# Query bound moved from ScalarE to VectorE, and one large SiLU with its reduction cut into eight, in a transformer layer on eight cores

## The chip, the cores and the metric

The kernel runs on one Trainium2 chip, on all 8 of its cores. Each core computes two of the sixteen sequences by itself; there is no exchange between cores. The metric is the device time of the slowest core, in microseconds (us), lower is better.

## The reference

The layer is an attention block and a feed-forward block, each between two layer norms, for x of shape (16, 2048, 1024). Cut to what matters:

```python
q, k, v = x@wq + bq, x@wk + bk, x@wv + bv              # 16 heads of 64
att = softmax(q @ k.T / 8) @ v
x = x + layernorm(att @ wo.T + bo)                     # x was layernorm(x) before q, k, v
# feed-forward on layernorm(x):
h = bit_linear(x, w1)                                  # 1024 -> 4096, x quantised per token, w1 ternary
h = silu(depthwise_conv1d(h, conv_w, conv_b))          # 3 taps along the sequence
# bit_linear's act_quant: scale = 127 / clip(max |h| over 4096); round(h * scale)
x = x + layernorm(bit_linear(h, w2))                   # 4096 -> 1024
```

## The kernel before, in words

Each core does a weight statistic once (`_p0`), and then for each of its two sequences: layer norm (`_p1_ln1`), the q, k and v projections (`_p2_qkv`), attention (`_p3_attn`), output projection and two layer norms (`_p4_proj_ln`), weight quantisation (`_p45_wquant`) and the feed-forward (`_p5_ffn`). Every stage writes one stream of instructions per engine. `em.emit` appends an instruction to its engine's stream with the semaphore values that it waits for, and every VectorE and ScalarE instruction also waits for the one before it on its own engine. The order on an engine is the order of the `emit` calls, and nothing reorders it.

**Attention (from line 439).** Heads go one after the other. In a head, 16 key blocks (`kt`) times 2 query halves (`j`) pass through a chain: scores on TensorE into `sc0` or `sc1` (line 514), exponential on ScalarE into `pt` (line 527), product with v on TensorE into `atps` (line 540). A score block waits for the exponential that last read its buffer. The exponential needs an upper bound of the scores, which comes from |q|: `emit_absq` (line 481) puts |q| of the next head into `absq`, `emit_M` (line 487) multiplies it with the maxima of |k|, and VectorE writes the negated bound into row 64 of `qa` (line 497). `absq` is the tile `oddh`, which also holds the finished output of odd heads (`ctx["absq"] = oddh`).

When a head ends, VectorE copies `atps` to `ivr`, which is the tile `ivfm` (line 549), and takes the reciprocal of its row 64, the softmax sums (line 557). The rest of the old head's work stands in the next head ahead of `kt` 7: `emit_post(h - 1)` (line 563) spreads the reciprocals over 64 partitions by TensorE (line 570) into `sc0` and `sc1`, and VectorE multiplies (line 581). For an even old head the product goes to `attn` (printed as `s_big`), for an odd one to `oddh`, from where a DMA moves it into `attn` (line 585, semaphore `sod`). `emit_absq(h + 1)` stands right behind this, and the score block of `kt` 7 waits for the multiplies (`mult_done`).

**Feed-forward (from line 789).** The sequence goes in 16 tiles of 128 tokens. In a tile, 32 blocks of 128 channels are computed: 8 matmuls per block on TensorE (line 842) into one of two PSUM tiles `hps`, which VectorE scales into `hgr` (line 854). TensorE can be two blocks ahead, since it waits for `hevac[idx - 2]`. After every fourth block VectorE does the convolution of these four in six operations (lines 879 to 889) into 512 of the 4096 columns of `tcv`. When all eight groups are done, ScalarE does SiLU on the whole of `tcv` (line 891), VectorE takes the maximum of the absolute value over the 32 blocks (line 893), and the scale comes from it by way of TensorE (lines 896 to 917). Then GpSimd and VectorE quantise the eight groups, and TensorE multiplies each with `w2q` (line 958).

## Time and profile before

| What | us |
|---|---|
| Runs: median of 2, and both | 7871.88 (7823.92, 7919.83) |
| The profiled execution, its own time | 7823.42 |
| Its span, first to last instruction, slowest core | 7821.4 |
| Shortest span of the eight cores | 7791.7 |
| VectorE busy, slowest core | 4261.6 |
| TensorE busy | 3709.8 |
| ScalarE busy | 1264.3 |
| GpSimd busy | 674.7 |

The profiled execution is 2 us outside its span and 48 us under the median of the two runs. The eight cores do the same work, and their spans lie within 30 us. No engine is busy for much over half of the span, so shares of busy time alone do not say what bounds the kernel; the stages have different limits and have to be read one by one.

### The profile page before, as it was taken

To read this page: it belongs to the slowest core of one execution; us is meant where nothing else is said; L and a number is where in the kernel's file an instruction comes from. 1 tells how busy PE (TensorE), PEld (TensorE's weight loads), DVE (VectorE), ACT (ScalarE), POOL (GpSimd) and SP (SyncE) were. 2 spreads that over 40 slices of the span, in tenths; PEclk is the share of its full clock that TensorE was granted. 3 is DMA by queue.
4 is the path that set the end of the run, shared out by engine and by line. 5 is a ranking of instruction groups with operands and counts; after the bars stand their busy time and mean duration, and the time that the engine had idled before them with its cause. 6 is when DMAs were issued, how large, how long until landed. Compare 5 with 4: busy or idle time off the path is not lost. (4 is left out here: it accounts for less than half of the span.)

```text
span 7821.4 us, 57703 instructions; the slowest of 8 cores (7791.7 to 7821.4 us)
## 1 busy us (share of the span) xinstructions
PE 3709.8 (47%) x17510; PEld 1786.6 (23%) x17510; DVE 4261.6 (54%) x5764; ACT 1264.3 (16%) x1226; POOL 674.7 (9%) x629
## 2 busy tenths in 40 slices
PE   0688787221144344344416887872224444344441
PEld 0322222110132232222203222221112222222220
DVE  4333443557666666666653334345546666666665
ACT  0046665000000000000000466650000000000000
POOL 0000000000012112112110000000002112112121
PEclk9987777565566666666658877775656666666665
DMA  6200000113400000000042000001120000000004
GB/s 191 60 6 6 9 9 5 50 38 110 158 6 6 3 6 6 3 6 3 6 156 52 7 5 8 9 5 50 38 97 6 3 6 4 5 6 3 6 6 132
DMA packets 59118, 251.86 MB, mean 32 GB/s; under 512 B 6720, under 2 KB 6848, under 8 KB 55232
## 3 DMA queue, kind: packets, MB, share of 16 engines
q1 hardware_dynamic: 40992, 197.32, 8.0%
q0 software_dynamic: 17824, 50.86, 2.4%
q8 instruction: 147, 2.41, 0.1%
q14 instruction: 155, 1.27, 0.1%
HBM read 185.77 MB, written 67.11 MB: 32 GB/s over the span
## 5 line engine op out<-in xcount | busy, mean ns | idle before, releaser
L842 PE MATMUL s_hps<-s_xqfm,s_w1q 128*128 128x130 bf16 (+1 forms) x8192 | 866.6, 293 | 1142.8 <-DVE s_hgr L854 768.8
L527 ACT ACTIVATE s_pt<-s_sc 128x1024 bf16<-128x1024 f32 x1024 | 1048.7, 1024 | 470.4 <-PE s_sc L514 401.5
L842 PEld LDWEIGHTS s_hps<-s_xqfm,s_w1q 128*128 128x128 bf16 x8192 | 777.9, 134 | 1240.0 <-issue 1219.6
L958 PE MATMUL s_fp<-s_w2q,s_gq 128*128 128x512 bf16 x2048 | 715.5, 512 | 713.8 <-DVE s_gq L947 713.8
L514 PE MATMUL s_sc<-s_qa,s_ka 65*128 65x512 bf16 x2048 | 774.4, 470 | 176.7 <-ACT s_pt L527 64.6
L540 PE MATMUL s_atps<-s_pt,s_vsb 128*65 128x512 bf16 x2048 | 691.8, 436 | 0.2 <-ACT s_pt L527 0.2
L891 ACT ACTIVATE s_tcv<-s_tcv 128x4096 bf16<-128x4096 bf16 x32 | 115.7, 3616 | 3454.7 <-DVE s_tcv L889 3454.7
L941 DVE SCALAR_TENSOR_TENSOR s_f<-s_db,s_r 128x512 f32<-128x512 f32 x256 | 395.6, 1545 | 406.9 <-POOL s_db L938 406.9
L929 POOL TENSOR_TENSOR s_yb<-s_tcv,s_sgb 128x512 f32<-128x512 bf16 x256 | 296.0, 1156 | 3539.4 <-DVE s_sgb L917 3507.3
L854 DVE SCALAR_TENSOR_TENSOR s_hgr<-s_hps,iwcol,s_ivfm 128x130 bf16<-128x130 f32 (+1 forms) x1024 | 361.4, 353 | 430.8 <-PE s_hps L842 371.4
L549 DVE COPY s_ivfm<-s_atps 65x2048 f32<-65x2048 f32 x32 | 73.2, 2286 | 845.2 <-PE s_atps L540 845.2
L958 PEld LDWEIGHTS s_fp<-s_w2q,s_gq 128*128 128x128 bf16 x2048 | 227.0, 119 | 1188.5 <-issue 1106.5
L557 DVE RECIPROCAL s_ivfm<-s_ivfm 1x2048 f32<-1x2048 f32 x32 | 414.2, 12944 | 3.3
L938 POOL TENSOR_TENSOR s_db<-s_yb,s_r 128x512 f32<-128x512 f32 x256 | 323.0, 1262 | 616.5 <-DVE s_r L935 616.5
L514 PEld LDWEIGHTS s_sc<-s_qa,s_ka 65*128 65x128 bf16 x2048 | 170.9, 108 | 742.8 <-issue 728.5
L540 PEld LDWEIGHTS s_atps<-s_pt,s_vsb 128*65 128x65 bf16 x2048 | 258.2, 127 | 312.2 <-issue 149.2
L716 PE MATMUL s_trp<-eye16s,s_xqt 128*128 128x128 bf16 x256 | 32.4, 306 | 604.2 <-DVE s_xqt L260 604.2
L893 DVE TENSOR_REDUCE s_gmax<-s_tcv 128x128 f32<-128x4096 bf16 x32 | 223.5, 6986 | 128.8 <-ACT s_tcv L891 128.8
L896 PE MATMUL s_tmp<-eye32s,s_gmax 128*128 128x128 f32 x32 | 14.3, 447 | 511.2 <-DVE s_gmax L893 511.2
L375 PE MATMUL s_qps<-s_big,s_xqfm 128*128 128x512 bf16 x1024 | 224.6, 383 | 39.5 <-DMA s_xqfm<-wq_t 39.5
L244 ACT ACTIVATE sdc<-st 128x1 f32<-128x1 f32 x128 | 25.9, 203 | 1159.1 <-DVE st L239 1159.0
L667 PE MATMUL s_op<-s_wo,s_big 128*128 128x512 bf16 x512 | 176.5, 521 | 41.1 <-DMA s_wo<-wo_t 41.1
(118 smaller groups left out, 3698.1 us busy)
## 6 DMA issues: line engine op xcount, KB each, us to landing
s_xint<-x SPq DMA_DIRECT2D x64, 512.0 KB, 4.1
p0st<-w_t SPq DMA_DIRECT2D x8, 2048.0 KB, 10.0
p0st<-w_t SPq DMA_DIRECT2D x32, 512.0 KB, 3.7
x2scr<-s_x2t SPq DMA_DIRECT2D x32, 512.0 KB, 2.9
s_wst<-w_t SPq DMA_DIRECT2D x16, 1024.0 KB, 5.1
s_wst<-w_t SPq DMA_DIRECT2D x32, 512.0 KB, 3.7
fscr<-s_ft POOLq DMA_DIRECT2D x32, 512.0 KB, 3.0
s_frl<-fscr SPq DMA_DIRECT2D x32, 512.0 KB, 5.9
```

The lines of the kernel that those rows point to most:

```text
L375: wo=wofs[wb]: e.matmul(ps[:, nb * 512:(nb + 1) * 512], wtens[:, wo + dc * D + oc * 128:wo + dc * D + oc * 128 + 128], xn1[:, dc * S + nb ...
L514: em.emit("tensor", lambda e, kt=kt, nb=nb, b=b, j=j: e.matmul(scp[j][:, nb * 512:(nb + 1) * 512], ka[:, b * S + kt * 128:b * S + kt * 128 ...
L527: em.emit("scalar", lambda e, p=p, j=j: e.activation(pt[:, p * S + j * Q:p * S + (j + 1) * Q], scp[j][:], AF.Exp), waits=w)
L540: em.emit("tensor", lambda e, kt=kt, nb=nb, h=h, p=p, j=j: e.matmul(atps[0:65, j * Q + nb * 512:j * Q + (nb + 1) * 512], vsb[:, kt * VW + ...
L557: em.emit("vector", lambda e: e.reciprocal(ivr[64:65, :], ivr[64:65, :]))
L842: j0=j0, j1=j1, t0=t0: e.matmul(ps[:, j0:j1], w1q[:, dc * DH + cc * 128:dc * DH + cc * 128 + 128], xqfm[:, dc * S + t0 + j0:dc * S + t0 + j1],
L854: t0=t0: e.scalar_tensor_tensor(hgr[:, gb + c4 * 130 + j0:gb + c4 * 130 + j1], ps[:, j0:j1], sb["iwcol"][:, 0:1], ivfm[:, t0 + j0:t0 + j1] ...
L893: em.emit("vector", lambda e: e.tensor_reduce(gmax[:], rearr(tcv, "p (c t) -> p t c", c=HC), AX.X, ALU.max, apply_absolute_value=True), wa ...
L929: em.emit("gpsimd", lambda e, ts=ts: e.tensor_tensor(rearr_ap3(yb), rearr_ap3(ts), sgv, ALU.mult), inc=ctx["gc"], waits=yw)
L938: em.emit("gpsimd", lambda e: e.tensor_sub(db2[:], yb[:], r02[:]), inc=ctx["gc"], waits=[(dv, r0d)])
L941: em.emit("vector", lambda e: e.scalar_tensor_tensor(f12[:], db2[:], 1.5, r02[:], ALU.is_gt, ALU.add), waits=[(ctx["gc"], dg)])
L958: gq4=gq4, cc4=cc4: e.matmul(ps[:, nb * 512:(nb + 1) * 512], gq4[:, cc4 * 128:(cc4 + 1) * 128], w2q[:, cc * D + nb * 512:cc * D + (nb + 1) ...
```

## The change

In attention, |q| is no longer one ScalarE activation (`Abs`) but two VectorE operations, a multiplication by -1 and a maximum. They stand at the same place in the order of the code, with the same waits for the DMAs `sqa` and `sod`. `emit_M` waits for a named exponential of the head before instead of for the newest ScalarE instruction. After the reciprocal, VectorE also copies row 64 to a bf16 row `ivb16` in the tile `xqfm`; nothing reads this copy, and the matmul of line 570 still reads the fp32 row with `ones32`. The new tile `ones16` isn't read either.

In the feed-forward, SiLU and the maximum are done per group of 512 columns, right behind the group's convolution: eight activations and eight reductions instead of one of each, and seven maxima that join the partial results. The two lines about `silu_ac` near the end give the variable the value that it had.

```diff
+    sb["ones16"] = nc.alloc_sbuf_tensor("ones16", [128, 128], BF16)
...
+                    ctx["ivb16"] = xqfm
...
-            em.emit("scalar", lambda e, b=b: e.activation(
-                absq[0:64, :], qa[0:64, b * S:(b + 1) * S], AF.Abs),
-                waits=[(sqa, None), (sod, None), (dv, None)])
+            em.emit("vector", lambda e, b=b: e.tensor_scalar_mul(
+                absq[0:64, :], qa[0:64, b * S:(b + 1) * S], -1.0),
+                waits=[(sqa, None), (sod, None)])
+            em.emit("vector", lambda e, b=b: e.tensor_tensor(
+                absq[0:64, :], absq[0:64, :], qa[0:64, b * S:(b + 1) * S],
+                ALU.max))
...
-                    waits=([(dv, None), (ac, None)] if nb == 0 else []))
+                    waits=([(dv, None), (ac, exp_cnt.get((h - 1, NT - 1, j), 0))]
+                           if nb == 0 else []))
...
             em.emit("vector", lambda e: e.reciprocal(
                 ivr[64:65, :], ivr[64:65, :]))
+            em.emit("vector", lambda e: e.tensor_copy(
+                ctx["ivb16"][64:65, 0:S], ivr[64:65, :]))
...
                     convd.append(dv.n)
-            em.emit("scalar", lambda e: e.activation(tcv[:], tcv[:], AF.Silu),
-                    waits=[(dv, None)])
-            em.emit("vector", lambda e: e.tensor_reduce(
-                gmax[:], rearr(tcv, "p (c t) -> p t c", c=HC), AX.X, ALU.max,
-                apply_absolute_value=True), waits=[(ac, None)])
+                    g_ = cc // 4
+                    em.emit("scalar", lambda e, g_=g_: e.activation(
+                        tcv[:, g_ * 512:(g_ + 1) * 512],
+                        tcv[:, g_ * 512:(g_ + 1) * 512], AF.Silu),
+                        waits=[(dv, None)])
+                    em.emit("vector", lambda e, g_=g_: e.tensor_reduce(
+                        gmax[:] if g_ == 0 else f12[:, 0:128],
+                        bass.AP(tcv, g_ * 512, [[HC * 128, 128], [1, 128],
+                                                [128, 4]]),
+                        AX.X, ALU.max, apply_absolute_value=True),
+                        waits=[(ac, None)])
+                    if g_ > 0:
+                        em.emit("vector", lambda e: e.tensor_max(
+                            gmax[:], gmax[:], f12[:, 0:128]))
...
+            del silu_ac
+            silu_ac = ctx["ac"].n
```

VectorE's order in the feed-forward, one group of a tile, before (the brackets name the semaphores that an instruction waits for: `pe` TensorE, `dv` VectorE, `ac` ScalarE):

```order
L854 SCALAR_TENSOR_TENSOR s_hgr<-s_hps,iwcol,s_ivfm 128x130 [waits pe,dv] x4
L879 TENSOR_TENSOR s_tcv<-s_hgr,cw_sb 128x512 [waits dv]
L881 TENSOR_TENSOR s_tcv<-s_tcv,cb_sb 128x512 [waits dv]
L883 TENSOR_TENSOR s_tmpg<-s_hgr,cw_sb 128x512 [waits dv]
L885 TENSOR_TENSOR s_tcv<-s_tcv,s_tmpg 128x512 [waits dv]
L887 TENSOR_TENSOR s_tmpg<-s_hgr,cw_sb 128x512 [waits dv]
L889 TENSOR_TENSOR s_tcv<-s_tcv,s_tmpg 128x512 [waits dv]
L854 SCALAR_TENSOR_TENSOR s_hgr<-s_hps,iwcol,s_ivfm 128x130 [waits pe,dv] x4
```

The same group in the changed kernel, whose lines are numbered differently (863 for 854, 888 to 898 for 879 to 889):

```order
L863 SCALAR_TENSOR_TENSOR s_hgr<-s_hps,iwcol,s_ivfm 128x130 [waits pe,dv] x4
L888 TENSOR_TENSOR s_tcv<-s_hgr,cw_sb 128x512 [waits dv]
L890 TENSOR_TENSOR s_tcv<-s_tcv,cb_sb 128x512 [waits dv]
L892 TENSOR_TENSOR s_tmpg<-s_hgr,cw_sb 128x512 [waits dv]
L894 TENSOR_TENSOR s_tcv<-s_tcv,s_tmpg 128x512 [waits dv]
L896 TENSOR_TENSOR s_tmpg<-s_hgr,cw_sb 128x512 [waits dv]
L898 TENSOR_TENSOR s_tcv<-s_tcv,s_tmpg 128x512 [waits dv]
L905 TENSOR_REDUCE s_f<-s_tcv 128x128 [waits ac,dv]
L912 TENSOR_TENSOR s_gmax<-s_gmax,s_f 128x128 [waits dv]
L863 SCALAR_TENSOR_TENSOR s_hgr<-s_hps,iwcol,s_ivfm 128x130 [waits pe,dv] x4
```

A reduction that waits for ScalarE, and a maximum, have come between the convolution of one group and the first read of `hps` of the next.

VectorE's order in attention from the start of an odd head (the copy out of `atps` of the even head before it) to the multiplies, before:

```order
L549 COPY s_ivfm<-s_atps 65x2048 [waits pe,dv]
L497 TENSOR_SCALAR s_qa<-s_sc 1x1024 [waits pe,dv] x2
L467 COPY s_qa<-s_qpk 64x2048 [waits dv]
L467 COPY s_ka<-s_kpk 64x2048 [waits dv]
L475 TENSOR_REDUCE s_mke<-s_ka 64x1 [waits dv]
L557 RECIPROCAL s_ivfm<-s_ivfm 1x2048 [waits dv]
L581 TENSOR_TENSOR s_big<-s_ivfm,s_sc 64x1024 [waits pe,dv] x2
```

And in the changed kernel, where 556 stands for 549, 504 for 497, 470 for 467, 478 for 475, 564 for 557 and 590 for 581:

```order
L556 COPY s_ivfm<-s_atps 65x2048 [waits pe,dv]
L504 TENSOR_SCALAR s_qa<-s_sc 1x1024 [waits pe,dv] x2
L470 COPY s_qa<-s_qpk 64x2048 [waits dv]
L470 COPY s_ka<-s_kpk 64x2048 [waits dv]
L478 TENSOR_REDUCE s_mke<-s_ka 64x1 [waits dv]
L564 RECIPROCAL s_ivfm<-s_ivfm 1x2048 [waits dv]
L566 CAST s_xqfm<-s_ivfm 1x2048 [waits dv]
L590 TENSOR_TENSOR s_big<-s_ivfm,s_sc 64x1024 [waits pe,dv] x2
L487 TENSOR_SCALAR s_oddh<-s_qa 64x2048 [waits dv]
L490 TENSOR_TENSOR s_oddh<-s_oddh,s_qa 64x2048 [waits dv]
```

The copy (L566) has come between the reciprocal and the multiplies, and the two operations that make |q| stand behind the multiplies. In the heads where the old head is odd, the first of these two waits for `sqa` and `sod` as well. On ScalarE nothing but exponentials is left in this stage.

## Rows read from the trace of the kernel before

**Rows 1.** The page's busy time, share of the span and instructions of each engine.

```profile
PE 3709.8 (47%) x17510; PEld 1786.6 (23%) x17510; DVE 4261.6 (54%) x5764; ACT 1264.3 (16%) x1226; POOL 674.7 (9%) x629
```

**Rows 2.** Windows, first sequence: attention, feed-forward. Columns: us, then busy per engine, PEclk, DMA share.

```profile
453.00:1382.00 929.00, 731.25 (x2240) 236.83 (x2240) 372.31 (x129) 556.20 (x529) 4.11 (x2) 0.78 0.03 7
2088.00:3835.00 1747.00, 741.66 (x4719) 467.52 (x4717) 1102.11 (x1787) 55.52 (x16) 298.55 (x254) 0.66 0.02 7
```

**Rows 3.** Timeline, feed-forward group and tile's end: start, us, engine, line, operation, idle before.

```profile
2671.39 3.63 PE L842 MATMUL s_hps<-s_xqfm,s_w1q 128*128 128x130 bf16 x32 [3.64 <-DVE s_hgr L854]
2672.59 0.35 DVE L854 SCALAR_TENSOR_TENSOR s_hgr<-s_hps,iwcol,s_ivfm 128x130 bf16<-128x130 f32 x1 [0.89 <-PE s_hps L842]
...
2707.05 0.43 DVE L889 TENSOR_TENSOR s_tcv<-s_tcv,s_tmpg 128x512 bf16<-128x512 bf16 x1
2707.62 3.62 ACT L891 ACTIVATE s_tcv<-s_tcv 128x4096 bf16<-128x4096 bf16 x1 [114.82 <-DVE s_tcv L889]
2711.41 6.99 DVE L893 TENSOR_REDUCE s_gmax<-s_tcv 128x128 f32<-128x4096 bf16 x1 [3.93 <-ACT s_tcv L891]
2718.54 0.45 PE L896 MATMUL s_tmp<-eye32s,s_gmax 128*128 128x128 f32 x1 [15.84 <-DVE s_gmax L893]
```

**Rows 4.** Groups of instructions by line and shape: busy us, mean ns, idle before.

```profile
L893 DVE TENSOR_REDUCE s_gmax<-s_tcv 128x128 f32<-128x4096 bf16 x32 | 223.5, 6986 | 128.8 <-ACT s_tcv L891 128.8
L885 DVE TENSOR_TENSOR s_tcv<-s_tcv,s_tmpg 128x512 bf16<-128x512 bf16 x256 | 108.7, 425 | 27.6 <-DVE s_tmpg L883 1.4
L201 DVE TENSOR_REDUCE t1c<-p0st 128x1 f32<-128x1024 f32 x32 | 39.0, 1220 | 39.9 <-DMA p0st<-w_t 39.8
L201 DVE TENSOR_REDUCE t1c<-p0st 128x1 f32<-128x4096 f32 x8 | 35.4, 4420 | 38.6 <-DMA p0st<-w_t 38.6
L253 DVE CAST s_qi<-s_yq 128x1024 int32<-128x1024 f32 x32 | 22.2, 694 | 3.6 <-DVE s_yq L712 0.5
L891 ACT ACTIVATE s_tcv<-s_tcv 128x4096 bf16<-128x4096 bf16 x32 | 115.7, 3616 | 3454.7 <-DVE s_tcv L889 3454.7
L484 ACT ACTIVATE s_oddh<-s_qa 64x2048 bf16<-64x2048 bf16 x32 | 61.1, 1909 | 217.0 <-DMA s_big<-s_oddh 133.6 <-DVE s_big L581 83.2
```

**Rows 5.** Line 484, what ended ScalarE's idle time before it: us in total, times.

```profile
  DMA s_big<-s_oddh: 133.6, 14
  DVE s_big L581: 83.2, 14
```

**Rows 6.** Timeline of attention, an even head (old head odd), around `kt` 7.

```profile
712.22 1.01 PE L514 MATMUL s_sc<-s_qa,s_ka 65*128 65x512 bf16 x2 [1.54 <-DVE s_oddh L581]
715.15 1.91 ACT L484 ACTIVATE s_oddh<-s_qa 64x2048 bf16<-64x2048 bf16 x1 [8.65 <-DMA s_big<-s_oddh]
724.13 14.41 ACT L527 ACTIVATE s_pt<-s_sc 128x1024 bf16<-128x1024 f32 x13 [0.21 <-PE s_sc L514]
739.46 2.29 DVE L549 COPY s_ivfm<-s_atps 65x2048 f32<-65x2048 f32 x1 [27.39 <-PE s_atps L540]
```

**Rows 7.** Timeline of attention, the odd head behind it (old head even).

```profile
750.52 12.94 DVE L557 RECIPROCAL s_ivfm<-s_ivfm 1x2048 f32<-1x2048 f32 x1
758.09 6.61 ACT L527 ACTIVATE s_pt<-s_sc 128x1024 bf16<-128x1024 f32 x6 [0.38 <-PE s_sc L514]
764.84 4.20 PE L570 MATMUL s_sc<-s_ivfm,ones 1*64 1x512 f32 x8 [1.21 <-ACT s_pt L527]
770.58 1.91 ACT L484 ACTIVATE s_oddh<-s_qa 64x2048 bf16<-64x2048 bf16 x1 [5.88 <-DVE s_big L581]
775.00 17.76 ACT L527 ACTIVATE s_pt<-s_sc 128x1024 bf16<-128x1024 f32 x16 [0.28 <-PE s_sc L514]
```

**Rows 8.** Windows of the same even head: TensorE slow, then fast.

```profile
712.00:723.00 11.00, 8.25 (x20) 2.95 (x21) 0.07 (x1) 6.11 (x6) 0.00 (x0) 0.50 0.11 24
723.00:739.00 16.00, 15.08 (x62) 5.50 (x60) 0.00 (x0) 14.23 (x14) 0.00 (x0) 0.99 0.00 1
```

**Rows 9.** Timeline, the end of the first sequence's attention.

```profile
1373.92 7.05 PE L570 MATMUL s_sc<-s_ivfm,ones 1*64 1x512 f32 x8 [15.65 <-DVE s_ivfm L557]
```

More of the change, by code:

```diff
@@ L180, in _p0 @@
     em.emit("gpsimd", lambda e: e.memset(sb["ones32"][:], 1.0))
+    em.emit("gpsimd", lambda e: e.memset(sb["ones16"][:], 1.0))
     em.emit("gpsimd", lambda e: e.memset(sb["epsc"][:], 1e-5))
```

## The prediction

> **What bounds the kernel now.** Busy time comes first: VectorE is busy for 54% of the span, TensorE for 47%, ScalarE for 16% [rows 1], so no engine bounds the whole. The windows of the two stages that the change touches are next [rows 2]. In attention ScalarE is busy for 556 of 929 us and TensorE for 731. In the feed-forward VectorE has 1102 of 1747 us, TensorE 742, ScalarE 56. The other stages are not touched; I count them at zero.
>
> The timeline then shows what waits for what. In the feed-forward TensorE does the 32 matmuls of a group in 3.63 us and has then waited 3.64 us for VectorE to free `hps` [rows 3]. So groups are 7.27 us apart, all of it VectorE's, and TensorE has half of it as slack. At the tile's end there is a chain with nothing beside it: convolution ends at 2707.48, SiLU starts 0.14 us later, takes 3.62, VectorE starts the reduction 0.17 us behind it, takes 6.99, and only then does TensorE go on [rows 3]. So whatever is put into VectorE's stream here is paid in full.
>
> In attention the limit alternates. With TensorE's granted clock at its upper level (2.4 GHz; 0.99 in the windows) ScalarE bounds: 13 exponentials take 14.41 us, so (14.41 - 1.02) / 12 = 1.116 us each [rows 6, 8]. After the stall at `kt` 7 the clock is at 0.50, 1.2 GHz [rows 8], and TensorE bounds, with four matmuls of 512 columns per exponential, 4 x 512 / 1.2 = 1.71 us.
>
> **The feed-forward, step by step.** What each tile loses from its end is 3.93 us of wait (with SiLU in it) and 6.99 us of reduction [rows 3], 10.92 us. What it gets:
>
> - SiLU of 512 columns. From 3616 ns for 4096 columns and 1909 for 2048 [rows 4] ScalarE takes 0.833 ns per column and 202 ns besides (another function, but the same engine and the same kind of operands): 629 ns. VectorE waits 0.14 + 0.63 + 0.17 = 0.94 us for it. The reduction stands right behind in VectorE's order, and so nothing of VectorE lies beside the wait. 8 x 0.94 = 7.51 us.
> - The reduction of 512 columns to 128. This is the term that no row shows. Contiguous reductions take 1220 ns for 1024 and 4420 ns for 4096 elements [rows 4]: 1.042 ns per element and 153 ns besides. The one of line 893 has 4096 elements too, but takes 6986 ns, 2566 more [rows 4]. It differs in two things: it reads with a step of 256 bytes, and it writes 128 results instead of one. If the step is what costs, an element takes (6986 - 153) / 4096 = 1.668 ns and the small reduction 153 + 512 x 1.668 = 1.01 us. If each result costs 2566 / 128 = 20 ns, it takes 153 + 533 + 2566 = 3.25 us. If neither returns with rows of four, 0.69 us. I take 1.01: both reductions read with the same step, and it is the only reading by which the total of the elements prices both. 8 x 1.01 = 8.06 us. The ends 0.69 and 3.25 are kept.
> - Seven maxima of 128 fp32 elements. The nearest rows are the 425 ns of a bf16 operation on 512 [rows 4] as the upper end, and 153 ns, the fixed part, as the lower. At one element per 1.042 ns it is 0.29 us, with the usual 0.11 us to the next instruction 0.40. 7 x 0.40 = 2.77 us.
>
> The gap of 0.11 us behind the convolution is there before and after. Sum per tile: 7.51 + 8.06 + 2.77 - 10.92 = +7.42 us. Two sequences of 16 tiles: 32 x 7.42 = +237 us. TensorE gives nothing back. It has the next two blocks ready and then waits for `hps`, as now, and the 0.89 us that VectorE waits for the third block [rows 3] comes after VectorE's own read and stays. The clock is already low in this phase (32 matmuls of 130 columns in 3.63 us, 113 ns each, near 130 / 1.2 = 108). By the ends of the reduction it is 32 x (8 x 0.69 - 0.64) = +156 us and 32 x (8 x 3.25 - 0.64) = +812 us.
>
> A page bears on this term. The Trainium skill, SBUF — State Buffer, section "Door 1: The DMA port swizzle", says in a note on cachelines that SBUF has lines of 16 bytes and that an access which crosses to a new line pays a penalty. By that rule every element of either reduction pays, and the small one takes 1.01 us; the 1.668 ns against 1.042 of the trace agree with a price per access, but do not prove it, since the number of results fits as well.
>
> **Attention, step by step.** The activation on |q| leaves ScalarE in the 28 heads where it stands behind a post. The two kinds differ.
>
> - Old head odd, 14 times: ScalarE can't take |q| until the DMA out of `oddh` has landed, at 715.15, though TensorE has restarted at 712.22 and has scores for it [rows 6]. The eighth exponential behind the stall starts at 724.13 + 2 x 1.116 = 726.36, 14.1 us after the restart. With an old even head there is no DMA to wait for, |q| starts when the multiplies are done and TensorE restarts too, and the eighth exponential comes at 775.00 + 5 x 1.116 = 780.58, 10.0 us after 770.58 [rows 7]. Without the activation the first kind can do no worse than the second: 4.1 us less. Some of that is the DMA and the activation, the rest that TensorE isn't interrupted while its clock is low. 14 x 4.1 = 58 us. The mean idle time before the activation, 133.6 / 14 = 9.5 us against 83.2 / 14 = 5.9 us [rows 5], differs by 3.6 us and supports the size.
> - Old head even, 14 times: about nothing. TensorE has just restarted at the low clock and is the bound, so the activation was hidden beside it: the third exponential comes 4.4 us after the restart [rows 7], and TensorE alone needs 1.2 + 2 x 1.71 = 4.6 at the low clock.
> - The first head of each sequence, 2 times, gains some 1.5 us: 3 us.
>
> VectorE's two operations take about 0.7 and 1.2 us (a bf16 operation with two inputs takes 425 ns for 512 elements [rows 4], (425 - 153) x 4 + 153 = 1.24). They stand where VectorE is idle for over 20 us, until `atps` is complete (27.39 us [rows 6]), and there its wait for the DMA is hidden too, as nothing is queued behind it but that copy. If that cover were gone it would be 2 us in each head, 60 us.
>
> The unread copy of the reciprocals stands on the path to the post. The cast of 1024 fp32 elements takes 694 ns [rows 4], so 2048 take 153 + 2 x 541 = 1.23 us, with the gap 1.34. The upper bound is the 2.29 us of the copy from PSUM [rows 6]. The reciprocal ends at 763.46, the exponentials for which the post also waits at 764.70 [rows 7]: 1.24 us of cover, so about 0.1 us is lost in the 14 or so heads of this kind, 2 us. Where the old head is odd there is more cover, since two copies are missing ahead of the reciprocal. At the end of a sequence the post waits for the reciprocal alone [rows 9]: 2 x 1.34 = 3 us. The changed wait of `emit_M` gives nothing, since its `dv` wait includes the copy out of `atps`, which comes after the last exponential anyway.
>
> Attention: -58 - 3 + 2 + 3 = -56 us. Its bounds are wide on one side: 20 us less gain if the clock's recovery doesn't follow, and up to 96 us more (the third rival).
>
> **Sum.** +237 - 56 = +181 us on the profiled execution's 7823.4: 8004 us. That execution lies 48 us under the median of the two runs, and the same sum on the median gives 8053. I forecast 8028, the middle, which is slower by 2.3% of 7823. A measurement of this kernel can tell about 2% from no change, which is 156 us, so the forecast lies only just outside.
>
> **Rivals.**
>
> - Each result of a reduction costs 20 ns. For it: the same 2566 ns. Against it: a cost of 19 VectorE cycles for one result is much for an engine that streams. The feed-forward gives +812, the whole 7823 + 812 - 56 = 8579 us. Chance 0.12.
> - Rows of four run at the contiguous rate. For it: four elements may be fetched differently from 32. Against it: the step is the same. The small reduction takes 0.69 us, and the whole comes to 7823 + 156 - 56 = 7923 us, within 2%. Chance 0.10. The Trainium skill, VectorE: DVE Perf Modes, section "The perf-mode tier table", says that `tensor_reduce` runs at one element per cycle in any memory; by that the small one takes 0.69 us. The trace agrees for line 201 and departs from it for line 893.
> - Not slower: TensorE's clock no longer falls at the stall. ScalarE frees the chain earlier, and if the clock stays up from the restart on, five steps at the low clock (1.71 us against 1.116) become fast in each head, 3 us. 32 x 3 = 96 us more than in the forecast: 7908 us, 1% over before, no difference that counts. It decides from 25 us (0.8 us a head) on. Against it: in the window from 712 to 723 the clock is low already at the restart [rows 8], and the post ahead of it is not shortened. Chance 0.04. Nothing that I can find makes the kernel faster by 2%; for that the feed-forward would have to be unchanged and attention to gain nearly three times its 56 us.
> - The forecast, 0.74.
>
> **How the numbers follow.** Inside the forecast the uncertainty is some 25 us, mostly the clock in attention and which execution is taken as the base; this puts about 0.06 of its 0.74 within 2%. Slower: 0.68 + 0.12 = 0.80. Within 2%: 0.06 + 0.10 + 0.04 = 0.20, less 0.01 for a gain unknown to me. The range goes from 7915, which takes in the second rival, to 8130, and leaves the first out.
>
> **What would show it.** In the changed profile the reductions of 512 elements take 1.01 us (3.25 or 0.69 for the rivals); SiLU takes 0.63 with 0.94 us of idle time ahead of each reduction; the distance between groups in a tile is 7.27 + 0.94 + 1.01 + 0.11 + 0.29 = 9.6 us; attention is 28 us shorter per sequence, and ScalarE's idle time at `kt` 7 of an even head falls from 8.65 to some 6.9 us, since the first exponential comes 1.2 us behind TensorE's restart. The forecast is wrong if SiLU and convolution overlap, if the clock at the restart is 1.00, or if groups are less than 9.3 us apart.

## The result and the profile after

The changed kernel takes 8043.5 us (median of 11 runs, 8024.8 to 8132.6) against 7841.3 (median of 10 runs of the kernel before). The ratio is 1.025, with 1.021 to 1.029 as its interval: slower by 2.5%. The forecast was 8028 us in a range from 7915 to 8130. The profiled execution took 8077.5 us. In it cores 4 to 7 had a lower granted clock (0.674 to 0.677) than cores 0 to 3 (0.691 to 0.694) and took some 45 us longer, for a reason that no run shows, so I compare cores 0 to 3. Core 0's span went from 7821.4 to 8004.6 us, +183.

The page's busy time, of core 6, beside [rows 1]:

```profile
PE 3777.3 (47%) x17510; PEld 1807.2 (22%) x17510; DVE 4463.4 (55%) x6308; ACT 1248.7 (15%) x1418; POOL 675.9 (8%) x630
```

VectorE is busy for 202 us more. That this is near the whole difference is chance, for the new waits for SiLU aren't in it, and in attention VectorE's new work is mostly hidden. The windows of core 0 (attention of the first sequence, a stretch of its feed-forward; columns as in [rows 2]) show TensorE's clock as before, and VectorE in attention with 40 us more, ScalarE with 31 less:

```profile
453.00:1377.00 924.00, 734.14 (x2237) 233.49 (x2236) 412.19 (x170) 525.09 (x513) 0.87 (x1) 0.78 0.04 9
2060.00:4095.00 2035.00, 793.08 (x5072) 501.50 (x5072) 1250.68 (x2205) 80.93 (x131) 321.27 (x276) 0.65 0.03 10
```

The groups of instructions of core 0, by line and shape (busy us, mean ns, idle time before), answer to [rows 4]:

```profile
L905 DVE TENSOR_REDUCE s_f<-s_tcv 128x128 f32<-128x512 bf16 x224 | 227.3, 1015 | 213.9 <-ACT s_tcv L901 213.9
L901 ACT ACTIVATE s_tcv<-s_tcv 128x512 bf16<-128x512 bf16 x256 | 161.0, 629 | 3776.8 <-DVE s_tcv L898 3776.7
L912 DVE TENSOR_TENSOR s_gmax<-s_gmax,s_f 128x128 f32<-128x128 f32 x224 | 65.5, 292 | 23.6 <-DVE s_f L905 0.5
L566 DVE CAST s_xqfm<-s_ivfm 1x2048 bf16<-1x2048 f32 x32 | 39.0, 1218 | 3.3
L490 DVE TENSOR_TENSOR s_oddh<-s_oddh,s_qa 64x2048 bf16<-64x2048 bf16 x32 | 39.0, 1217 | 3.3
L905 DVE TENSOR_REDUCE s_gmax<-s_tcv 128x128 f32<-128x512 bf16 x32 | 32.5, 1015 | 33.2 <-ACT s_tcv L901 33.2
L487 DVE TENSOR_SCALAR s_oddh<-s_qa 64x2048 bf16<-64x2048 bf16 x32 | 21.9, 685 | 44.9 <-DMA s_big<-s_oddh 42.9
```

The small reduction takes 1.015 us, SiLU 0.63, and VectorE waits (213.9 + 33.2) / 256 = 0.965 us for it each time. The maxima take 0.29. The end of one group of the feed-forward in the timeline of core 0 (start, us, then as in [rows 3]) shows them in a row:

```profile
2224.99 0.42 DVE L898 TENSOR_TENSOR s_tcv<-s_tcv,s_tmpg 128x512 bf16<-128x512 bf16 x1
2225.57 0.63 ACT L901 ACTIVATE s_tcv<-s_tcv 128x512 bf16<-128x512 bf16 x1 [9.00 <-DVE s_tcv L898]
2226.37 1.01 DVE L905 TENSOR_REDUCE s_f<-s_tcv 128x128 f32<-128x512 bf16 x1 [0.95 <-ACT s_tcv L901]
2227.49 0.29 DVE L912 TENSOR_TENSOR s_gmax<-s_gmax,s_f 128x128 f32<-128x128 f32 x1
2227.88 0.81 DVE L863 SCALAR_TENSOR_TENSOR s_hgr<-s_hps,iwcol,s_ivfm 128x130 bf16<-128x130 f32 x2
2228.38 1.89 PE L851 MATMUL s_hps<-s_xqfm,s_w1q 128*128 128x130 bf16 x16 [6.00 <-DVE s_hgr L863]
```

Between the end of the convolution, 2225.41, and the next read of `hps`, 2227.88, lie 2.47 us with nothing of VectorE's other work in them. The groups are 9.62 us apart, and TensorE's wait for `hps` has grown from 3.64 [rows 3] to 6.00 us: it is still the engine with slack.

An even head around `kt` 7 (timeline of core 0, answers to [rows 6]):

```profile
692.06 3.94 PE L579 MATMUL s_sc<-s_ivfm,ones 1*64 1x512 f32 x8 [1.21 <-ACT s_pt L534]
697.88 1.01 PE L521 MATMUL s_sc<-s_qa,s_ka 65*128 65x512 bf16 x2 [1.89 <-DVE s_oddh L590]
699.05 1.02 ACT L534 ACTIVATE s_pt<-s_sc 128x1024 bf16<-128x1024 f32 x1 [7.13 <-PE s_sc L521]
700.80 0.69 DVE L487 TENSOR_SCALAR s_oddh<-s_qa 64x2048 bf16<-64x2048 bf16 x1 [3.06 <-DMA s_big<-s_oddh]
702.40 17.75 ACT L534 ACTIVATE s_pt<-s_sc 128x1024 bf16<-128x1024 f32 x16 [0.62 <-PE s_sc L521]
```

The DMA now holds up VectorE, which has nothing else to do. ScalarE starts with an exponential 1.17 us behind TensorE's restart; before, it waited 2.93 us for the DMA and then did |q| first. Its idle time is 7.13 us instead of 8.65. The windows behind this restart (columns as in [rows 2]) show the other half of the gain:

```profile
697.90:699.90 2.00, 2.00 (x5) 0.75 (x6) 0.00 (x0) 0.85 (x1) 0.00 (x0) 0.50 0.48 104
699.90:701.90 2.00, 2.00 (x6) 0.84 (x5) 1.00 (x2) 1.20 (x2) 0.00 (x0) 0.50 0.12 27
701.90:703.90 2.00, 1.98 (x9) 0.76 (x8) 0.90 (x1) 1.41 (x2) 0.00 (x0) 0.96 0.03 8
```

TensorE works without a gap from the restart and is back at 2.4 GHz (0.96 in the window) after 4 us. In the head of [rows 6], on the kernel before, it took 10 us, with two of them idle (windows of that kernel):

```profile
716.20:718.20 2.00, 0.00 (x0) 0.00 (x0) 0.00 (x0) 1.88 (x2) 0.00 (x0) 0.50 0.00 0
722.20:724.20 2.00, 2.00 (x8) 0.83 (x7) 0.00 (x0) 1.10 (x3) 0.00 (x0) 0.71 0.00 0
```

To see where the time went I took the length of each stage from its first and last record: attention from the first copy of keys and queries to the last multiply, the feed-forward from the first read of `hps` to the last write of its output, both sequences together.

| stage, us | before (8 cores) | after (cores 0 to 3) | difference | forecast |
|---|---|---|---|---|
| feed-forward | 3810 to 3819, median 3814 | 4060 to 4064, median 4061 | +247 | +237 |
| attention | 1859 to 1865, median 1862 | 1819 to 1829, median 1824 | -38 | -56 |
| all the rest | 2118 to 2144 | 2106 to 2125 | some -15 | 0 |

The rest moved by as much among kernels in which nothing of it differs (2105 to 2145 us on cores 0 to 3 of all runs), so I take the -15 for the noise of an execution. Attention is 18 us short of its forecast. Per core, an even head (counted from 0; from its first exponential to that of the next head, in the mean of heads 2 to 14) went from 58.5-58.9 to 54.5-54.7 us, as forecast (4.1 less); an odd one (heads 1 to 13) from 54.4-54.6 to 56.1-56.75. Before, an odd head needed 5.8 to 6.1 us from the post's first matmul to the restart of the chain; now 6.8 to 7.4, again in the mean of a core.

### The profile page after: what moved, and what is told of

It reads as the page before. It is cut to its first block and busy times, and to the rows that moved or that the text cites. A ratio compares the mean times of both kernels' runs of the same rounds, so it can differ in the third digit from the quotient of the medians.

```text
span 8075.8 us, 59576 instructions; the slowest of 8 cores (7990.8 to 8075.8 us)
## 1 busy us (share of the span) xinstructions
PE 3777.3 (47%) x17510; PEld 1807.2 (22%) x17510; DVE 4463.4 (55%) x6308; ACT 1248.7 (15%) x1418; POOL 675.9 (8%) x630
## 5 line engine op out<-in xcount | busy, mean ns | idle before, releaser
L901 ACT ACTIVATE s_tcv<-s_tcv 128x512 bf16<-128x512 bf16 x256 | 161.2, 630 | 3778.3 <-DVE s_tcv L898 3778.3
L905 DVE TENSOR_REDUCE s_f<-s_tcv 128x128 f32<-128x512 bf16 x224 | 227.0, 1014 | 213.9 <-ACT s_tcv L901 213.9
L378 PE MATMUL s_qps<-s_big,s_xqfm 128*128 128x512 bf16 x1024 | 247.9, 411 | 38.0 <-DMA s_xqfm<-wq_t 38.0
L579 PE MATMUL s_sc<-s_ivfm,ones 1*64 1x512 f32 x256 | 182.0, 872 | 74.9 <-DVE s_xqfm L566 51.2
```

The costliest lines, as they stand in the source:

```text
L378: wo=wofs[wb]: e.matmul(ps[:, nb * 512:(nb + 1) * 512], wtens[:, wo + dc * D + oc * 128:wo + dc * D + oc * 128 + 128], xn1[:, dc * S + nb ...
L905: em.emit("vector", lambda e, g_=g_: e.tensor_reduce(gmax[:] if g_ == 0 else f12[:, 0:128], bass.AP(tcv, g_ * 512, [[HC * 128, 128], [1, 128],
```

## The experiments

All ratios are to the kernel before, run on the same chip, with the 95% interval behind them. Ranges of a stage are over the eight cores where nothing else is said.

**The two parts apart.** `e3_attention_only` is the changed kernel with the old end of the tile:

```diff
-                    g_ = cc // 4
-                    em.emit("scalar", lambda e, g_=g_: e.activation(
-                        tcv[:, g_ * 512:(g_ + 1) * 512],
-                        tcv[:, g_ * 512:(g_ + 1) * 512], AF.Silu),
-                        waits=[(dv, None)])
...
+            em.emit("scalar", lambda e: e.activation(tcv[:], tcv[:], AF.Silu),
+                    waits=[(dv, None)])
+            em.emit("vector", lambda e: e.tensor_reduce(
+                gmax[:], rearr(tcv, "p (c t) -> p t c", c=HC), AX.X, ALU.max,
+                apply_absolute_value=True), waits=[(ac, None)])
```

> Only the attention part of the change; the feed-forward is that of the kernel before. If the two parts don't act on each other: attention about 1820 us for both sequences (1861 before), feed-forward 1905 us each as before, the kernel 0.5% faster than before (ratio 0.995). If the attention gain of the changed kernel belongs to something else (placement in memory, clock of a die), it stays at 1.000.

Measured 7789.8 us, 0.995 (0.993 to 0.997); attention 1817 to 1836 us, feed-forward 3805 to 3818.

`e4_ffn_only` is the kernel before with that part of the change alone, the reverse of the diff above.

> Only the feed-forward part of the change. Theory: the eight exposed waits, reductions and maxima cost 247 us per core by themselves; feed-forward 2030 us per sequence, attention as before, ratio 1.031. Rival: part of the 247 us comes from the rest of the change (the lower clock of a die, memory placement); then it is under 1.028.

Measured 8048.7 us, 1.027 (1.025 to 1.029); feed-forward 4057 to 4065 us, attention 1854 to 1865. So each part moves its own stage and leaves the other where it was. -0.5% and +2.7% add to +2.2%, beside 2.5% (2.1 to 2.9) for the whole. For the second I had expected 1.031, and had named a ratio under 1.028 as a sign that part of the 247 us comes from elsewhere. The ratio is under it, but the feed-forward grew by its 246 us all the same (4060 against 3814); in the profiled execution it is the untouched stages that were some 15 us shorter again.

**The copy of the reciprocals.** `e1_no_copy` takes it out:

```diff
             em.emit("vector", lambda e: e.reciprocal(
                 ivr[64:65, :], ivr[64:65, :]))
-            em.emit("vector", lambda e: e.tensor_copy(
-                ctx["ivb16"][64:65, 0:S], ivr[64:65, :]))
             ctx[f"_iv{h}"] = dv.n
```

> The changed kernel without the unread bf16 copy of the reciprocals. What is asked: why attention became only 38 us shorter per core (both sequences, undisturbed die) where 56 were forecast. Heads with an even number became 4.3 us shorter, odd ones 1.9 to 2.3 us longer. Theory A: in odd heads the copy ends up to 1.2 us after the exponentials for which the post also waits, and this delay is enough that TensorE's clock is at its lower level for the post, so the copy costs more than its own uncovered time. Then odd heads go back from 56.5 to some 54.5 us, attention (both sequences) from about 1820 to about 1790 us, and the kernel is 2.1% slower than before instead of 2.5%. Rival B: the copy costs only the 0.1 us of the forecast, and attention stays within 5 us of 1820. Rival C: the two |q| operations on VectorE lengthen the odd heads; they stay at 56.5 us.

`e2_copy_behind` keeps it, but emits it in `emit_post`, behind the multiplies:

```diff
             mult_done[h] = dv.n
+            em.emit("vector", lambda e: e.tensor_copy(
+                ctx["ivb16"][64:65, 0:S], ivr[64:65, :]))
```

> The changed kernel with the same copy moved behind the post's multiplies, where VectorE is idle. Theory A (the copy's place between reciprocal and post is what costs): as without the copy, odd heads 54.5 us, attention about 1790 us. If instead the copy costs wherever it stands (VectorE's time, or the write to that tile), attention stays at about 1820 us.

Measured: 7992.9 us, 1.0215 (1.0174 to 1.0256), without the copy, and 7990.1, 1.0193 (1.0175 to 1.0211), with it behind the multiplies. The first interval overlaps that of the changed kernel (1.021 to 1.029), the second ends at its edge. The stages say more: attention is 1793 to 1799 us on cores 0 to 3 of the first and 1793 to 1796 on all cores of the second, against 1819 to 1829. So the copy costs some 30 us where it stands, and nothing where it runs beside TensorE. It is the place, not the 1.22 us of VectorE. Most of it is in the odd heads, 54.8-55.0 us in the first and 54.6-54.9 in the second against 56.1-56.75: 14 x 1.5 = 21 us. The even heads have 0.2 us each, some 3 us, and the first and last heads of the sequences the rest.

How does 1.22 us cost that much, where 0.1 was forecast? An odd head of the changed kernel, core 0 (timeline):

```profile
844.57 12.94 DVE L564 RECIPROCAL s_ivfm<-s_ivfm 1x2048 f32<-1x2048 f32 x1
849.04 8.83 ACT L534 ACTIVATE s_pt<-s_sc 128x1024 bf16<-128x1024 f32 x8 [1.54 <-PE s_sc L521]
857.62 1.22 DVE L566 CAST s_xqfm<-s_ivfm 1x2048 bf16<-1x2048 f32 x1
859.09 7.05 PE L579 MATMUL s_sc<-s_ivfm,ones 1*64 1x512 f32 x8 [2.28 <-DVE s_xqfm L566]
862.91 1.21 DVE L590 TENSOR_TENSOR s_big<-s_ivfm,s_sc 64x1024 bf16<-64x1024 f32 x1 [4.07 <-PE s_sc L579]
866.32 1.21 DVE L590 TENSOR_TENSOR s_big<-s_ivfm,s_sc 64x1024 bf16<-64x1024 f32 x1 [2.20 <-PE s_sc L579]
867.68 1.01 PE L521 MATMUL s_sc<-s_qa,s_ka 65*128 65x512 bf16 x2 [1.54 <-DVE s_big L590]
...
4729.02 12.94 DVE L564 RECIPROCAL s_ivfm<-s_ivfm 1x2048 f32<-1x2048 f32 x1
4736.90 6.60 ACT L534 ACTIVATE s_pt<-s_sc 128x1024 bf16<-128x1024 f32 x6 [0.68 <-PE s_sc L521]
4742.07 1.22 DVE L566 CAST s_xqfm<-s_ivfm 1x2048 bf16<-1x2048 f32 x1
4743.64 3.89 PE L579 MATMUL s_sc<-s_ivfm,ones 1*64 1x512 f32 x8 [1.20 <-ACT s_pt L534]
4745.71 1.21 DVE L590 TENSOR_TENSOR s_big<-s_ivfm,s_sc 64x1024 bf16<-64x1024 f32 x1 [2.43 <-PE s_sc L579]
4747.71 1.21 DVE L590 TENSOR_TENSOR s_big<-s_ivfm,s_sc 64x1024 bf16<-64x1024 f32 x1 [0.78 <-PE s_sc L579]
4749.07 1.01 PE L521 MATMUL s_sc<-s_qa,s_ka 65*128 65x512 bf16 x2 [1.53 <-DVE s_big L590]
```

In the first head the exponentials are done at 857.87, but the copy only at 858.84. The post starts 1.22 us behind the exponentials, after 2.28 us of idle TensorE, and takes 7.05 us; in the second head, 0.14 us behind them, 3.89. From the post to the restart it is 8.59 us in the one and 5.43 in the other. The windows of the two posts (columns as in [rows 2], the clock third from the end) show why:

```profile
859.10:863.10 4.00, 4.00 (x5) 1.15 (x6) 0.19 (x1) 0.00 (x0) 0.00 (x0) 0.50 0.00 0
863.10:867.70 4.60, 3.06 (x5) 0.50 (x4) 2.29 (x3) 0.00 (x0) 0.00 (x0) 0.50 0.00 0
4743.50:4747.20 3.70, 3.56 (x8) 0.98 (x8) 1.21 (x1) 0.00 (x0) 0.00 (x0) 0.95 0.00 0
```

The late post runs at the low level of TensorE's clock, 1.2 GHz, the punctual one mostly at 2.4. The 112 odd heads of the eight cores sort the same way; the mean granted clock during the post is 0.84 in the 46 punctual ones and 0.54 in the 66 others:

| post behind the last exponential | heads | post to restart, us | head, us |
|---|---|---|---|
| up to 0.3 us | 46 | 5.80 | 54.85 |
| 0.3 to 1.0 us | 25 | 7.72 | 57.71 |
| 1.0 to 1.5 us | 41 | 8.33 | 58.16 |

Heads whose post starts 1.0 to 1.5 us behind (1.19 in the mean, where 0.14 is the least) take 3.3 us longer. But neither lateness nor idle time fixes the price by itself. On cores 0 to 3 of this kernel 76 posts behind some 1.2 us of idle TensorE take from 3.89 to 6.08 us, 27 of them over 5, and in `e2_copy_behind` odd heads need 6.3 to 6.65 us from post to restart, where the kernel before needed 5.8 to 6.1, although every post is punctual in both. No run here shows what decides the moment at which the clock falls.

`e9_quarter_copy` makes the copy short and `e10_copy_twice` makes it twice as long:

```diff
-                ctx["ivb16"][64:65, 0:S], ivr[64:65, :]))
+                ctx["ivb16"][64:65, 0:512], ivr[64:65, 0:512]))
```

> The changed kernel with the copy cut to 512 of its 2048 columns (0.42 + 0.11 us instead of 1.22 + 0.11). In odd heads the reciprocal ends about as long ahead of the last exponential as the whole copy takes, so this one should be fully covered if the cost lies in the post starting late: attention near the 1794 us without the copy (within 8), odd heads 54.5 to 55 us. If any instruction between reciprocal and post costs, whatever its length (an extra semaphore step, the other tile), it stays near 1824 us, odd heads 56 us.

```diff
             em.emit("vector", lambda e: e.tensor_copy(
                 ctx["ivb16"][64:65, 0:S], ivr[64:65, :]))
+            em.emit("vector", lambda e: e.tensor_copy(
+                ctx["ivb16"][64:65, 0:S], ivr[64:65, :]))
```

> The changed kernel with the same copy done twice in a row, 2.65 us between reciprocal and post. If the post starting late is the cause, odd heads grow by at least the 1.33 us of the second copy over the changed kernel's 56.5 us, to 57.8 or more, and even heads (cover about 2.8 us) stay within 0.5 us of 54.6: attention 1824 + 14 x 1.33 + 3 = about 1846 us. If the cost came only once from TensorE's clock being low at the post, and not from lateness itself, the second copy costs less than 1 us per head.

There is one execution of each, 8017.8 and 8075.2 us, so I go by the stages. Attention takes 1794 to 1810 us (median 1802) with the quarter, 1859 to 1875 (median 1868) with two: in order of the copy's length (none, a quarter, one, two) 1795, 1802, 1824, 1868. With the quarter 65 odd heads are on time and take 54.6 us, 47 are 0.4 us late and take 55.8. With two copies 87 are 2.36 us late and take 58.7, the other 25 are 1.26 us late and take 57.6 (6.73 us from post to restart, less than the 8.33 of the heads that are 1.19 us late with one copy). So both rivals fall: it is not any instruction whatever its length, and the second copy costs more than 1 us per odd head. It costs 44 us, twice what I expected of it: odd heads lose 2.0 us instead of 1.33, and even heads, which I had taken as covered (at most 0.5 us), about 1 us. The direction is shown by four lengths; the size is not a constant per microsecond.

**The step of the reduction.** `e5_steps` is the kernel before, in which the reduction still reads 4096 elements for 128 results, but with a step that changes from tile to tile, so that the maximum is taken over other columns:

```diff
-            em.emit("vector", lambda e: e.tensor_reduce(
-                gmax[:], rearr(tcv, "p (c t) -> p t c", c=HC), AX.X, ALU.max,
+            em.emit("vector", lambda e, i=i: e.tensor_reduce(
+                gmax[:], bass.AP(tcv, 0, [[HC * 128, 128], [1, 128],
+                                         [2 ** (i % 8), 32]]), AX.X, ALU.max,
```

> The kernel before with another access pattern in the one large maximum of the feed-forward: 128 results of 32 elements each, always 4096 elements, but the step between the elements of a result is 1, 2, 4, 8, 16, 32, 64 or 128 elements of 2 bytes, by the tile's number modulo 8, instead of 128. The maximum is taken over the wrong columns, so its value is not the reference's. Theory (the step costs): steps of a few bytes take 153 + 4096 x 1.042 = 4420 ns, the large ones 6986 ns, and somewhere between 2 and 256 bytes it changes. Rival (each of the 128 results costs 20 ns, and rows of four are exempt from it for a reason unknown): 6986 ns at every step.

There is one execution, 7786.5 us. The timeline of core 6, tiles with steps of 1, 4, 8, 16 and 32 elements of 2 bytes:

```profile
2108.06 4.42 DVE L893 TENSOR_REDUCE s_gmax<-s_tcv 128x128 f32<-128x4096 bf16 x1 [5.22 <-ACT s_tcv L891]
2340.53 4.42 DVE L893 TENSOR_REDUCE s_gmax<-s_tcv 128x128 f32<-128x4096 bf16 x1 [3.93 <-ACT s_tcv L891]
2456.93 7.33 DVE L893 TENSOR_REDUCE s_gmax<-s_tcv 128x128 f32<-128x4096 bf16 x1 [3.93 <-ACT s_tcv L891]
2576.07 7.47 DVE L893 TENSOR_REDUCE s_gmax<-s_tcv 128x128 f32<-128x4096 bf16 x1 [3.94 <-ACT s_tcv L891]
2696.69 6.98 DVE L893 TENSOR_REDUCE s_gmax<-s_tcv 128x128 f32<-128x4096 bf16 x1 [3.93 <-ACT s_tcv L891]
```

128 results in 4.42 us: the same as one result of 4096 elements [rows 4]. So a result costs nothing, and the whole 2.57 us comes with the step. It begins between 8 bytes (4.42) and 16 bytes (7.33), and from 64 to 256 bytes the reduction takes 6.98 to 6.99. Every core shows the same durations in both sequences. The Trainium skill, SBUF — State Buffer, section "Door 1: The DMA port swizzle", which has 16-byte lines and a penalty for each new one, agrees with where the price begins. Why 16 and 32 bytes (7.33 and 7.47 us) cost more than longer steps stays open. With a longer step the reduction also reads more different elements (159 at a step of 1, 4096 at 128), and no run here parts the two; the jump of 2.91 us from a step of 4 to one of 8 elements, with hardly a further rise up to 128, speaks for the step.

**Giving the wait back.** `e6_reduce_a_group_later` is the changed kernel with the reduction of a group emitted behind the convolution of the next:

```diff
-                    em.emit("vector", lambda e, g_=g_: e.tensor_reduce(
...
-                        waits=[(ac, None)])
...
+                    silu_n = ctx["ac"].n
+                    for r_, n_ in ([(g_ - 1, prev_silu)] if g_ else []) + \
+                            ([(7, silu_n)] if g_ == 7 else []):
+                        em.emit("vector", lambda e, g_=r_: e.tensor_reduce(
...
+                            waits=[(ac, n_)])
+                        if r_ > 0:
+                            em.emit("vector", lambda e: e.tensor_max(
+                                gmax[:], gmax[:], f12[:, 0:128]))
+                    prev_silu = silu_n
```

> The changed kernel with the reduction and maximum of a group moved behind the convolution of the next group; only the eighth still stands right behind its SiLU. Theory: VectorE waits 0.97 us for each SiLU with nothing beside it, and seven of eight such waits go: 7 x (0.97 - 0.11) = 6.0 us per tile, 193 us per core; feed-forward 4060 -> 3868 us for both sequences (3812 before the change), ratio to before 1.000 instead of 1.025. Rival: the extra time is in the number of VectorE operations alone, and the waits only take the place of later waits for TensorE's blocks; then feed-forward stays over 4030 us.

Measured 7818.9 us, 0.999 (0.996 to 1.002), the feed-forward 3837 to 3841 us, 222 us less, so the rival (over 4030) falls. The timeline of core 0:

```profile
2306.07 0.42 DVE L898 TENSOR_TENSOR s_tcv<-s_tcv,s_tmpg 128x512 bf16<-128x512 bf16 x1
2306.60 1.02 DVE L908 TENSOR_REDUCE s_f<-s_tcv 128x128 f32<-128x512 bf16 x1
2307.73 0.29 DVE L915 TENSOR_TENSOR s_gmax<-s_gmax,s_f 128x128 f32<-128x128 f32 x1
2308.12 0.81 DVE L863 SCALAR_TENSOR_TENSOR s_hgr<-s_hps,iwcol,s_ivfm 128x130 bf16<-128x130 f32 x2
```

The reduction follows the convolution with the usual gap; the wait is gone, while both reduction and maximum still cost their time. I had expected 193 us, with the eighth SiLU bare. It isn't, since the reduction of group 7 lies beside it: 8 x (0.965 - 0.105) x 32 = 220.

**Better than both.** `e7_running_max` has no copy, and no reduction either. ScalarE writes |t| of each group, VectorE takes the maximum in bf16 over 512 columns, and only at the tile's end folds 512 columns to 128:

```diff
-                    em.emit("vector", lambda e, g_=g_: e.tensor_reduce(
...
+                    def join(n):
+                        em.emit("vector", lambda e: e.tensor_tensor(
+                            gqb[:, 0:512], gqb[:, 0:512], gqb[:, 512:1024],
+                            ALU.max), waits=[(ac, n)])
+                    if g_ >= 2:
+                        join(abs_n)
+                    em.emit("scalar", lambda e, g_=g_: e.activation(
+                        gqb[:, 512:1024] if g_ else gqb[:, 0:512],
+                        tcv[:, g_ * 512:(g_ + 1) * 512], AF.Abs),
+                        waits=[(dv, None)])
+                    abs_n = ctx["ac"].n
+                    if g_ == 7:
+                        join(abs_n)
+            em.emit("vector", lambda e: e.tensor_tensor(
+                gqb[:, 0:256], gqb[:, 0:256], gqb[:, 256:512], ALU.max))
+            em.emit("vector", lambda e: e.tensor_tensor(
+                gmax[:], gqb[:, 0:128], gqb[:, 128:256], ALU.max))
```

> A version that should beat both: attention of the changed kernel without the copy; SiLU per group, then |.| on ScalarE into a spare tile, and on VectorE a running maximum of 512 bf16 columns with unit step one group later, folded to 128 at the tile's end. Per tile: 7 joins of 0.425 + 0.105 = 3.7 us, a last wait for SiLU and |.| of 1.6 us, two folds 0.6 us, together 5.9 us where the kernel before has 11.0: feed-forward 3812 - 163 = 3649 us; attention 1794 us as without the copy; the kernel 0.970 of before. If ScalarE changes its table between SiLU and |.| (1.28 us each) the last wait is 2.9 us and feed-forward 3690. If the joins run at one element per cycle (692 ns), 3709.

Measured 7576.8 us, 0.968 (0.965 to 0.972), the feed-forward 3626 to 3633 us, 183 less than before. The end of a tile (timeline of core 0):

```profile
2291.53 0.42 DVE L905 TENSOR_TENSOR s_gq<-s_gq 128x512 bf16<-128x512 bf16 x1
2291.58 0.63 ACT L899 ACTIVATE s_tcv<-s_tcv 128x512 bf16<-128x512 bf16 x1 [6.45 <-DVE s_tcv L896]
2292.30 0.63 ACT L910 ACTIVATE s_gq<-s_tcv 128x512 bf16<-128x512 bf16 x1
2293.10 0.43 DVE L905 TENSOR_TENSOR s_gq<-s_gq 128x512 bf16<-128x512 bf16 x1 [1.14 <-ACT s_gq L910]
2293.63 0.29 DVE L917 TENSOR_TENSOR s_gq<-s_gq 128x256 bf16<-128x256 bf16 x1
2294.03 0.29 DVE L919 TENSOR_TENSOR s_gmax<-s_gq 128x128 f32<-128x128 bf16 x1
```

A join takes 0.43 us where reduction and maximum took 1.31. One wait for ScalarE is left, 1.14 us at the end of the tile, in place of 3.93 for the whole of SiLU; that it is not the 1.6 I expected is 15 of the 18 us that the stage came out under the expected 3649. The absolute value costs ScalarE 0.63 us, hidden but for the last one of a tile, and a switch between the two functions shows no gap beyond 0.09 us.

`e8_bf16_post` is the same kernel with the copy back where it was, and now read: the post's matmuls take `ones16` and `ivb16`.

```diff
-                        sb["ones32"][64:65, 0:64],
-                        ivr[64:65, j * Q + nb * 512:j * Q + (nb + 1) * 512],
+                        sb["ones16"][64:65, 0:64],
+                        ctx["ivb16"][64:65,
+                                     j * Q + nb * 512:j * Q + (nb + 1) * 512],
```

> The version with the running maximum, with the copy back in its place and now read: the post multiplies bf16 reciprocals with bf16 ones, four matmuls of 512 columns instead of eight passes in fp32. If the post's time follows TensorE (8 x 0.43 us before, 4 x 0.22 to 0.43 now), the stretch from post to restart falls from 6.4 to about 4.0 us in 30 heads, 70 us, of which the late copy takes back some 20: attention about 1745 us, ratio 0.964. If the delay by the copy in odd heads costs as much as in the changed kernel (30 us) and the multiplies on VectorE bound the post, attention stays within 10 us of 1794.

Measured 7524.5 us, 0.964 (0.959 to 0.969), the fastest of all. Attention is 1731 to 1734 us, some 63 less than in `e7_running_max`. The post still starts 1.14 us behind the last exponential in odd heads (mean of core 0), but reaches the restart in 3.77 us. The price is that the reciprocals are rounded to bf16. The intervals of the last two overlap; the stages show the 63 us plainly, on all eight cores.

## Why the prediction was right

The sum on the profiled execution was 8004 us and core 0 came out at 8004.6. That is better than its terms were, and partly luck: on core 0 the feed-forward came out 10 us over its term, attention 21 over, and the rest, which I had put at nothing, 29 under. The 8028 was these +181 on a base halfway between two, 7848, of which they are 2.3%; I put them down as 2.3% of 7823, from which 8028 is 2.6% away. That the runs of the kernel before would have their median at 7841, near this base, is luck too. The whole is 202 us slower by the medians, 21 more than the sum.

- **The wait for SiLU** (0.94 forecast): 0.965. Nothing of VectorE lay beside it, as said; [rows 3] already had both hand-overs in them. That these waits are what costs is shown by `e6_reduce_a_group_later`, where they go and 222 us with them.
- **The reduction** (1.01): 1.015, and SiLU 0.63 as from the line through two lengths. The choice among three readings was right; the steps show that the price goes with the step and not with the 128 results. Both rivals on this term fall: by results it would be 3.25 us, and at the contiguous rate 0.69. So does the perf-mode rule for this operation: the Trainium skill, VectorE: DVE Perf Modes, section "The perf-mode tier table", which has one element per cycle for it, holds for steps up to 8 bytes here, where 4096 elements take 4.42 us, and not from 16 bytes on.
- **The maxima** (0.29 and a gap of 0.11): 0.29 and 0.105. The sum of a tile by measured rows is 8 x 0.965 + 8 x 1.015 + 7 x 0.40 - (128.8 + 223.5) / 32 = +7.6 us, 32 times that +244, against +237 forecast and +247 in the stage. The groups are 9.62 us apart (9.6).
- **The even heads** (-4.1 each): -4.2. ScalarE's idle time at `kt` 7 is 7.13 us (6.9 forecast). VectorE's two operations take 0.69 and 1.22 us and cost at most some 0.3 us: without the copy odd heads take 54.6 to 55.0 us, before the change 54.4 to 54.6.
- **The rival of the clock** (it no longer falls at the stall) falls: in the even head it is at 0.50 at the restart and for 4 us behind it, and it is at 0.50 in the first microsecond behind the restart in all 112 even heads. That it comes back 6 us sooner than before, with TensorE no longer interrupted, is part of the 4.1 us and was counted there.
- **The step that failed** is the cost of the unread copy: "1.24 us of cover, so about 0.1 us is lost in the 14 or so heads of this kind, 2 us", with 3 us at the sequences' ends. It measured 30 us (1824 against 1794 and 1795). Two things were wrong in it. The cover was read from one head of the kernel before. It was a usual one there (median 1.22 us over 112 heads, 9 of them under 0.5), but the change speeds up the exponentials in front of that very post (the first 14 of an odd head took 18.45 us in the mean of cores 0 to 3, now 18.21), so that 38 heads have under 0.5 us of cover and in 66 of 112 the copy is what the post waits for. And a late post was priced by its lateness, while TensorE at the low clock takes up to 7.05 us for the eight matmuls, and 3.9 at best at the high one. Both durations stood in the rows the forecast was made from: 4.20 us in [rows 7], 7.05 behind 15.65 us of idle time in [rows 9]. They should have been compared. With this term at 30 us the sum for attention is -31, and -38 was measured.

One thing stays open: when exactly the clock falls in the gap before the post. Two heads of the same kernel, 1.20 and 2.28 us of idle time, come out differently, but so do posts with the same 1.2 us, and the runs that varied the gap by the copy's length give no point at which it falls. Nor do I explain the 19 us between the difference of the medians (+202) and that of core 0 (+183).

## What to carry to other kernels

Cutting a piece of work into eighths hides nothing if each eighth is consumed right behind its making, on an engine that works in order: eight waits of 0.965 us replaced one of 4.0. Emit the consumer one piece later (222 us back here), and reduce by whole-row maxima on two-byte data with unit step rather than by a strided reduction (0.43 against 1.31 us a group, with the absolute value moved to ScalarE, which had the time). When a small operation is put ahead of a wait on the critical path, take its cover from what the changed kernel will do there, and price the lateness with TensorE at the clock that it may have after the longer idle time: being a microsecond late cost 3.3 us here.

## What the hardware showed that was not expected

- A VectorE reduction of 4096 bf16 elements takes 4.42 us at steps of 2, 4 and 8 bytes, 7.33 at 16, 7.47 at 32, and 6.98 to 6.99 at 64, 128 and 256. So the longest steps are not the slowest.
- The same eight fp32 matmuls of one row take from 3.89 to 6.08 us when TensorE has idled some 1.2 us before them (76 posts on cores 0 to 3 of the changed kernel), and from 6.56 to 7.05 when it has idled 2.1 to 2.3 us (26 posts). But with two copies 23 posts behind 2.1 to 2.5 us take 4.91 to 5.65 us.
- Two copies of 1.22 us ahead of the post cost some 74 us of attention, one 30, a quarter of one 7 or 8: the second copy costs more than the first.
